# The normed x of five later pieces of work is turned by strided DMA through DRAM in place of TensorE

## The reference, cut to what matters

```python
xn = _layernorm(x)
x = x + _L0_attn_ref(xn, ...) + _L0_ffn_ref(xn, ...)
xn = _layernorm(x)
x = x + _L1_attn_ref(xn, ...) + _L1_ffn_ref(xn, ...)

def _L0_ffn_ref(x, Wg, Wu, Wd, Wr, Ag, Bg, Au, Bu, Ad, Bd):   # 8 experts of rank 16, the best 2 per token
    gate_base = xf @ Wg.T
    up_base = xf @ Wu.T
    base_out = jax.nn.silu(gate_base) * up_base @ Wd.T
    router_logits = xf @ Wr.T
    ...
def _L1_ffn_ref(x, w_gate, w_up, w_down):
    h = jax.nn.silu(x @ w_gate) * (x @ w_up)
    return _sparsify_2to4(h) @ w_down
```

## Time and profile before

| | |
|---|---|
| time, median of 2 runs | 722.21 us (719.66 to 724.76) |
| the profiled execution: its own time, its span | 726.31 us, 724.4 us |
| TensorE busy | 687.9 us, 95% of the span |
| VectorE busy | 517.9 us, 71% |
| ScalarE busy | 374.9 us, 52% |
| GpSimd busy | 138.6 us, 19% |
| DMA queue of SyncE | 20,576 packets, 23.79 MB, 10.0% of 16 engines |
| the chain of work that ended last | PE 69%, DVE 19%, issue 5%, ACT 4%, POOL 2%, DMA 1% |

### The profile page before, as it was taken

The page is one execution under the profiler, slowest core; times in us unless marked ns, Lnnn a source line. Parts: engine busy times, 40 slices in busy tenths (PEclk is TensorE's granted clock), DMA queues, the critical chain, the costliest instruction groups (busy, mean ns, idle before and its releaser), DMA issues.

```text
span 724.4 us, 10585 instructions
## 1 busy us (share of the span) xinstructions
PE 687.9 (95%) x4030; PEld 582.1 (80%) x4030; DVE 517.9 (71%) x933; ACT 374.9 (52%) x773; POOL 138.6 (19%) x129
## 2 busy tenths in 40 slices
PE   3899999969989999999999999999999999999997
PEld 2768888858868788887888878887687888888886
DVE  7726566874876466664666656666769998998997
ACT  4786777744754435444344443445656455354541
POOL 7543453510000001000010000100040323303220
PEclk9989999999999999999999999999999999999999
DMA  5085453000000000000000000050000000000000
GB/s 189 5 290 186 136 142 100 1 1 0 1 1 1 0 1 1 1 0 1 1 1 1 0 1 1 1 233 0 1 1 0 1 1 30 1 29 1 2 30 30
DMA packets 21282, 25.78 MB, mean 36 GB/s; under 512 B 976, under 2 KB 19408, under 8 KB 20464
## 3 DMA queue, kind: packets, MB, share of 16 engines
q1 hardware_dynamic: 20576, 23.79, 10.0%
q10 hardware_dynamic: 656, 1.31, 0.5%
HBM read 22.94 MB, written 2.16 MB: 35 GB/s over the span
## 4 chain that ended last, share of the span: by engine, by line
PE 69%; DVE 19%; issue 5%; ACT 4%; POOL 2%; DMA 1%; DVEq 0%; POOLq 0%; ACTq 0%
PE bank L89 21%; PE bank L91 19%; PE bank L90 19%; DVE l_ring_lo L2451 2%; PE bank L489 2%; DVE l_ge L2432 2%; DVE l_h L2447 2%; DVE l_o L2455 1%; DVE l_h L2404 1%; POOL m_den L825 1%; DVE h_raw L1173 1%; PE bank L465 1%; DVE m_st L903 1%; DVE h_ring_lo L1178 1%; PE bank L1395 1%
## 5 line engine op out<-in xcount | busy, mean ns | idle before, releaser
L1173 DVE TENSOR_TENSOR h_raw<-h_s,bank 128x512 f32<-128x512 f32 x104 | 71.4, 687 | 117.5 <-ACT h_s L1163 102.9
L1163 ACT ACTIVATE h_s<-bank 128x512 f32<-128x512 f32 x104 | 62.2, 598 | 161.6 <-PE bank L91 161.5
L1178 DVE TENSOR_TENSOR h_ring_lo<-h_raw,h_ring_hi 128x512 fp32r<-128x512 f32 x92 | 70.5, 766 | 0.1
L1167 ACT ACTIVATE h_ring_hi<-h_raw 128x512 fp32r<-128x512 f32 x104 | 64.7, 622 | 1.2 <-DVE h_raw L1173 1.2
L90 PE MATMUL bank<-fused_lo,h_ring_hi 128*128 128x256 f32 x208 | 58.8, 283 | 0.0
L89 PE MATMUL bank<-f_yT_hi,mlp_hi 128*128 128x512 f32 x128 | 51.6, 403 | 2.9 <-DVE h_raw L1173 2.9
L2152 ACT ACTIVATE l_s<-bank 128x512 f32<-128x512 f32 x32 | 19.1, 598 | 64.6 <-PE bank L91 64.6
L89 PE MATMUL bank<-l_xT_hi,l_wgu 128*128 128x512 f32 x128 | 51.3, 401 | 0.1
L90 PE MATMUL bank<-l_xT_lo,l_wgu 128*128 128x512 f32 x128 | 50.3, 393 | 0.0
L91 PE MATMUL bank<-l_xT_hi,l_lo 128*128 128x512 f32 x128 | 50.3, 393 | 0.0
L91 PE MATMUL bank<-f_yT_hi,fused_lo 128*128 128x512 f32 x128 | 50.2, 392 | 0.0
(11 more groups left out here) (362 smaller groups left out, 2021.5 us busy)
## 6 DMA issues: line engine op xcount, KB each, us to landing
m_W<-m_scratch SPq DMA_DIRECT2D x16, 512.0 KB, 5.8
fused_raw<-in_fused SPq DMA_DIRECT2D x1, 3584.0 KB, 15.6
res<-in_x SPq DMA_DIRECT2D x4, 512.0 KB, 6.0
fused_raw<-in_fused SPq DMA_DIRECT2D x2, 1024.0 KB, 8.2
l_raw<-in_layer SPq DMA_DIRECT2D x1, 2048.0 KB, 8.7
out_x<-res SPq DMA_DIRECT2D x16, 128.0 KB, 1.9
l_raw<-in_layer SPq DMA_DIRECT2D x1, 1280.0 KB, 11.3
fused_raw<-in_fused SPq DMA_DIRECT2D x1, 1152.0 KB, 5.1
```

The source lines that it names most:

```text
L1163: self.nc.scalar.activation(self.s[u % 2][r, :], gate[r, :], ACT.Silu).then_inc(self.silu.sem, 1)
L1167: self.nc.scalar.activation(self.unit(i, u)[0], self.product(i, u), ACT.Copy).then_inc(self.hi.sem, 1)
L1173: self.nc.vector.tensor_tensor(out=self.product(i, u), in0=self.s[u % 2][r, :], in1=up[r, :], op=ALU.mult).then_inc(self.hidden.sem, 1)
L1178: self.nc.vector.tensor_tensor(out=lo, in0=self.product(i, u), in1=f32(hi), op=ALU.subtract).then_inc(self.lo.sem, 1)
```

## The change

A DRAM tensor `tokens` is added, with 512 rows of 256 for each of eight pieces of x, and two views: `by_token` (partition = token) and `by_column` (partition = feature, the 512 tokens along the row, 256 elements apart in memory). For batches 1 to 3 of L0 and tiles 2 and 3 of L1, SyncE waits until xs is written, stores it to `tokens`, waits for that to land, and issues two loads (one for each 128 features) through `by_column` into `xw`, which lies over xs. ScalarE's `high_x` waits for both loads and reads `xw` in place of the banks; `low_x` too. The transposes of these five are gone, and the wait for `zprod` moves to `router_and_ranks`. `norm_x(i + 1)` moves from u = 15, 16 to u = 11, 12, ahead of `scale_y`. In L1 the norm of tile 2 moves from tile 1's body to tile 0's, behind the last `act_abs`, and that of tile 3 likewise to tile 1's; it now waits for `xT_lo` of the tile before. Batch 0 and tiles 0 and 1 are turned by TensorE as before.

```diff
@@ fused_phase, SyncE
+        for i in range(1, B):
+            sp.wait_ge(xs_ready.sem, xs_ready.at(i, 2))
+            sp.dma_start(g.by_token(i), xs[:, :, :]).then_inc(x_stored.sem, 16)
+            sp.wait_ge(x_stored.sem, x_stored.at(i - 1, 16))
+            for k in range(KD):
+                sp.dma_start(xw[:, k, :], g.by_column(i)[:, k, :], allow_slow_non_contiguous=True).then_inc(x_loaded.sem, 16)
         sp.wait_ge(hid.down.sem, hid.down.at(B - 1, NF))
@@ fused_phase, TensorE
-            if i:
-                pe.wait_ge(zprod.sem, zprod.at(i - 1, 2))
...
-                if u == 2:
+                if u == 2 and i == 0:
                     turn_x(i)
@@ fused_phase, ScalarE
         def high_x(i):
+            if i:
+                act.wait_ge(x_loaded.sem, x_loaded.at(i - 1, 32))
             for k in range(KD):
-                act.wait_ge(xT_t.sem, xT_t.at(i, k + 1))
-                nc.scalar.activation(xT[0][:, k, :], turn_bank[k][:, :], ACT.Copy).then_inc(xT_hi.sem, 1)
+                if i == 0:
+                    act.wait_ge(xT_t.sem, xT_t.at(i, k + 1))
+                nc.scalar.activation(xT[0][:, k, :], xw[:, k, :] if i else turn_bank[k][:, :], ACT.Copy).then_inc(xT_hi.sem, 1)
@@ fused_phase, VectorE
                     if u == 10:
                         mean_square(i + 1)
+                    elif u in (11, 12):
+                        norm_x(i + 1, u - 11)
                     elif u == 14:
                         scale_y(i + 1)
-                    elif u in (15, 16):
-                        norm_x(i + 1, u - 15)
@@ layer1_phase, SyncE
+        turned_x(2)
         for i in range(C):
+            if i == 1:
+                turned_x(3)
@@ layer1_phase, TensorE
-            turn_x(following)
+            if following == 1:
+                turn_x(following)
@@ layer1_phase, ScalarE
             exponentials(i)
-            if i and following is not None:
-                norm(following)
             act_silu(i, GP)
...
                 act_abs(i, GP + 3)
+                if following + 1 < C:
+                    norm(following + 1)
                 for j in range(GP):
                     act_hi(i, j)
```

More of the change, by code:

```diff
@@ L197, in program @@
         g.x_in, g.cols_in, g.bias_in = x_in, cols_in, bias_in
+        g.tokens = nc.dram_tensor("tokens", (B + C, S, D), fp32, kind="Internal").ap()
+        g.by_token = lambda n: g.tokens[n].rearrange("(c p) d -> p c d", p=P)
+        g.by_column = lambda n: g.tokens[n].rearrange("t (k p) -> p k t", p=P)
         l1 = layer1_weights(nc, g, layer1_in)
@@ L1320, in fused_phase @@
     over = Map(nc, spread_at)
+    xw = Map(nc, over.at)("f_xw", [P, KD, S])
     xs, ys = over("f_xs", [P, C, D]), over("f_ys", [P, C, D])
@@ L1345, in fused_phase @@
     xs_ready, xT_t, xT_hi, xT_lo = (sg("f_" + n, 2) for n in ("xs", "xTt", "xThi", "xTlo"))
+    x_stored, x_loaded = sg("f_xst", 16), sg("f_xld", 32)
     lg_ready, lg_copied, lgT, centred, exped = (sg("f_" + n, 1) for n in ("lg", "lgc", "lgT", "cent", "exp"))
@@ L1464, in router_and_ranks @@
             pe.wait_ge(xT_lo.sem, xT_lo.at(i, KD))
+            if i:
+                pe.wait_ge(zprod.sem, zprod.at(i - 1, 2))
             known_weights(i, "ranks")
@@ L1689, in low_x @@
                 dve.wait_ge(xT_hi.sem, xT_hi.at(i, k + 1))
-                nc.vector.tensor_tensor(out=xT[1][:, k, :], in0=turn_bank[k][:, :], in1=f32(xT[0][:, k, :]), op=ALU.subtract).then_inc(xT_lo.sem, 1)
+                nc.vector.tensor_tensor(out=xT[1][:, k, :], in0=xw[:, k, :] if i else turn_bank[k][:, :], in1=f32(xT[0][:, k, :]), op=ALU.subtract).then_inc(xT_lo.sem, 1)
         def low_ranks(i, n):
@@ L1933, in layer1_phase @@
     first, a_at, c_at, d_at = splitting.first, splitting.spots.a, splitting.spots.c, splitting.spots.d
+    xw = Map(nc, g.XN)("l_xw", [P, KD, S])
     xs, o = first.xs, first.spare("l_o", [P, L, D])
@@ L1954, in layer1_phase @@
     x_ready, xT_t, xT_hi, xT_lo = first.x_ready, first.xT_t, first.xT_hi, first.xT_lo
+    x_stored, x_loaded = sg("l_xst", 16), sg("l_xld", 32)
     zprod, zsum, zhi, zlo, back, back_added = rest.zprod, rest.zsum, rest.zhi, rest.zlo, rest.back, rest.back_added
@@ L1981, in _, with turned_x @@
     def _(sp):
+        def turned_x(i):
+            sp.wait_ge(x_ready.sem, x_ready.at(i, 1))
+            sp.dma_start(g.by_token(B + i), xs[:, :, :]).then_inc(x_stored.sem, 16)
+            sp.wait_ge(x_stored.sem, x_stored.at(i - 2, 16))
+            for k in range(KD):
+                sp.dma_start(xw[:, k, :], g.by_column(B + i)[:, k, :], allow_slow_non_contiguous=True).then_inc(x_loaded.sem, 16)
+        turned_x(2)
         for i in range(C):
+            if i == 1:
+                turned_x(3)
             for l in range(L):
@@ L2165, in norm @@
         def norm(i):
-            act.wait_ge(xT_t.sem, xT_t.at(i - 1, KD))
+            if i <= 2:
+                act.wait_ge(xT_t.sem, xT_t.at(i - 1, KD))
+            else:
+                act.wait_ge(xT_lo.sem, xT_lo.at(i - 1, KD))
             if i == 1:
@@ L2175, in high_x @@
         def high_x(i):
+            if i >= 2:
+                act.wait_ge(x_loaded.sem, x_loaded.at(i - 2, 32))
             for k in range(KD):
-                act.wait_ge(xT_t.sem, xT_t.at(i, k + 1))
-                nc.scalar.activation(xTs[i % 2][0][:, k, :], turn_bank[k][:, :], ACT.Copy).then_inc(xT_hi.sem, 1)
+                if i == 1:
+                    act.wait_ge(xT_t.sem, xT_t.at(i, k + 1))
+                nc.scalar.activation(xTs[i % 2][0][:, k, :], xw[:, k, :] if i >= 2 else turn_bank[k][:, :], ACT.Copy).then_inc(xT_hi.sem, 1)
         def copy_first(l):
@@ L2352, in low_x @@
                 dve.wait_ge(xT_hi.sem, xT_hi.at(i, k + 1))
-                nc.vector.tensor_tensor(out=xTs[i % 2][1][:, k, :], in0=turn_bank[k][:, :], in1=f32(xTs[i % 2][0][:, k, :]), op=ALU.subtract).then_inc(xT_lo.sem, 1)
+                nc.vector.tensor_tensor(out=xTs[i % 2][1][:, k, :], in0=xw[:, k, :] if i >= 2 else turn_bank[k][:, :], in1=f32(xTs[i % 2][0][:, k, :]), op=ALU.subtract).then_inc(xT_lo.sem, 1)
         def weigh_experts(n):
```

## The result

The changed kernel takes 932.26 us (median of 928.39 and 936.13) where the kernel before takes 722.21. The ratio is 1.2888, with an interval of 1.2809 to 1.2967: slower, by 210 us.

A forecast was written before the change was run, and what follows sets the result against it. TensorE, 95% busy, was taken to bound the kernel. From 724.4 us, less 5.3 for transposes, plus 96 (L0 waits), 81 (L1 waits) and 15 (slow clock), came 911 us of span, 909 us of time; range 760 to 1,620 us.

The forecast's parts named there:

- What bounds it, and the gain: TensorE, 95% busy, sets the end; removing five groups of eight transposes in L0 and L1 gains 5.3 us.
- The time left: From xs ready to its reader: 44.3 us in L0, 34.6 in L1; with cover 45 and 36.6.
- The packet: Each 4-byte element of the strided loads costs 8.8 ns on its engine: load 36 us, pair 72, chain 77.
- The lower bound of 5.5 ns: Strided loads: packet price with record overlap of 3.3 ns taken off, giving 22.5 us a load, 45 a pair.
- The clock and the cover: Slow TensorE clock adds 3 us after each of five waits, 15 us; TensorE's work covers 1 us (L0), 2 (L1).
- The sum: Whole kernel: 724.4 - 5.3 + 96 + 81 + 15 = 911 us of span, 909 us of time.
- The order: Norms moved ahead of the ring copies in L1 (2.07 us on ScalarE) cost 0, or 4 us if nothing covers them.
- A small packet costs as much as a 512-byte one: Rival on the strided loads: pair 213 us, chain 218, time 1,614 us; chance 0.17, shared with the skill page's price.
- Cheaper than the record: Rival on the strided loads: pair 45 us, chain 50, clock barely falls, time 764 us; chance 0.14.
- In between: Rival on the strided loads: scattered reads cost more than the record, pair 110 to 180 us, time 1,100 to 1,450; chance 0.20.
- Hidden: Rival: neighbours gathered or both loads in one's time (36 us), chain 41 us, time 726, or 717 if all hidden; chance 0.06.
- The estimate of 100 us a load: Strided loads by the skill page's factor of 19 over the crossbar: 200 us a pair, time about 1,550 us.

The follow-up runs named there:

- e3_run16: Changed kernel with loads in runs of 16 floats (64 bytes), x not turned: 719.74 us against 722.05 for the kernel before, ratio 0.9954.
- e1_order: Kernel before with the norms moved to where the change puts them, TensorE's transposes kept: 725.52 us against 722.05, ratio 1.0027.
- e5_first_layer: Changed kernel with the change in L0 alone, L1 as in the kernel before: 834.85 us, one execution.
- e4_two_queues: Changed kernel with the second load of each pair issued from ScalarE's queue: 938.4 us, one execution.
- e2_run2: Changed kernel with loads in runs of 2 floats (8 bytes), half the packets, x not turned: 737.42 us, one execution.
- e7_store_side: Changed kernel with the turning done by four stores of 4-byte pieces to DRAM, loads reading whole rows: 2,393.62 us, one execution.

## Why the prediction was right

Its steps, one by one.

**What bounds it, and the gain.** TensorE sets the end, and a wait ahead of it is added whole: the table of differences above gives 37.7 to 38.2 us for waits of 37.8 to 38.7, and 48.2 and 47.3 for the two of 47.8. The gain of 1.07 us a group was 1.0 (e3_run16).

**The time left.** Taken 44.3 us and 34.6 without cover. Measured: 83.1 - 38.7 = 44.4 from the store's issue to where ScalarE stood idle, and 753.80 - 671.43 - 47.70 = 34.7 in the second layer, whose store went out at 671.43. Both distances came from two rows of the old trace and held to 0.1 us.

**The store** landed in 2.8 us, 3 taken, and the loads followed at once. The rows that answer to the earlier trace rows:

```profile
tokens<-f_xs SPq DMA_DIRECT2D x3, 512.0 KB, 2.8
f_xw<-tokens SPq DMA_DIRECT2D x6, 256.0 KB, 60.1
```

The 60.1 is the median of loads that stand first in line (41.2 us) and second (79.6).

**The packet.** 8.8 ns was taken, and it is the term that was mis-sized: 9.5 ns in the middle of a pair, and over the pair, from its issue at 208.63 to 288.98, 80.4 us / 8,192 = 9.8 ns with the landing in it, where 74 us were taken. The chain is 83 us and not 77. The value lay close, but the step to it was weaker than it looks. The 8.8 ns were the length of a packet's record, and in the changed kernel the records are 1.80 times as long as the packets are apart: 1.801 x 9.5 = 17.1 ns. That the record of a small piece ahead of the work is near the distance of those in a full queue is luck; nothing in the old trace showed it. The lower bound of 5.5 ns, which took some overlap off, went the wrong way. The packet count was exact.

**The clock and the cover.** 15 us were taken for the slow clock behind five waits, less 3 x 0.7 + 2 x 2 = 6.1 of cover, for TensorE works on into the wait. From batch 0's start to the end e3_run16 takes 555.3 us and the kernel before 560.3, so the gain is 5.0; the changed kernel takes 767.5, which is 207.2 more. 207.2 + 5.0 - 210.0 = 2.2 us are left for clock less cover, where 8.9 were taken. The clock was taken rightly: worked out as the prediction did it, length times missing clock, the stretches behind the five waits (0.77, 0.76, 0.72, 0.65 and 0.76 over 11 to 12 us) give 15 us, an estimate. The cover was taken too small: it took some 13 us back and not 6, for TensorE was busy 2.6 to 2.7 us in each wait of the first layer and 4.9 and 4.4 us in those of the second.

**The sum.** Waits without cover: 3 x 32.7 + 2 x 42.4 = 182.9 expected, 210.0 measured, 27 more. Clock less cover: 2.2 in place of 8.9, 6.7 less. The early phase: 5.9 less, by chance of the execution, and no term of the sum. Together 911 + 27.1 - 6.7 - 5.9 = 925.5, and 0.3 for the gain, against a span of 925.7. So part of the closeness is luck, terms of both signs; with the packet's price alone set right, the span would have come out at 938. The other 8.8 us between 909 and 932 are not in the profile: the median was put 2.2 us below the span, as for the kernel before, and the median of the two executions, 7.7 us apart, lies 6.6 above it.

**The order** cost 0 (e1_order). **Waits add** (e5_first_layer).

**The rivals.** *A small packet costs as much as a 512-byte one* would have had a load of 106.5 us; it is 40. The argument for it, that 1.8 packets per ns over all engines were not to be had, is refuted: 118,039 in 70 us are 1.69 per ns, against 0.68 in the densest stretch of before. *Cheaper than the record* is refuted by the same number. *In between* (a pair of 110 us and more) too. *Hidden* fails in both its forms: neighbours are not gathered, since the count is one packet per element, and two loads don't run in the time of one (e4_two_queues). But its threshold, a pair of 40 us for the first layer, was right: with a pair of 41 us (e2_run2) the first layer no longer waits and the second still does.

The Trainium skill, page "VectorE: DVE Perf Modes", section "The three transpose paths", calls the strided copy a trap against the crossbar's transpose, which no run here has; against TensorE's turning, 0.5 us of the path, a load of 40 us bears the warning out. The estimate of 100 us a load, worked out in the prediction from its factor of 19, is 2.5 times what was measured. The section gives the factor for a large stride on the side written, which the prediction left out: the changed kernel writes SBUF without a gap and has its stride on the side read. In e7_store_side the side written has the stride, and the same 65,536 elements take 186 us, 1.9 times the estimate.

What the prediction didn't see is that the cure lies in the start of the chain. It took the place of the norm as given; the same packets, begun 42 us earlier and into space that is free by then, cost nothing in four of the five groups. The fifth, tile 2, was not run that way.

## What to carry to other kernels

A load that turns by strides costs its number of contiguous runs, here 9.0 to 9.6 ns for each on each of 16 engines, whether a run has 4, 8 or 64 bytes: count runs, divide by 16, multiply, and compare with the distance from the producer to the reader. If the chain is longer, the excess is paid once for each group; if the chain can be started early enough, it costs nothing, full DMA engines and all. And don't turn the pattern round without a measurement: the same number of 4-byte pieces cost 4.7 times as much when they were written to DRAM.

## What the runs showed of the hardware

- Scattered 4-byte writes from SBUF to DRAM come 45.1 ns apart on an engine, scattered 4-byte reads 9.5, 8-byte reads 9.0 and 64-byte reads 9.6. Neither theory of e7_store_side had it.
- The recorded length of a small packet is not its price. The engines' share reads 1.80 when full of 4-byte reads and 1.70 with the writes; the price is the time over the count.
- An issue behind such a load holds its engine: 39 us on SP for the second load, and 38.23 for an output behind it. On two queues each issue takes 0.6 to 0.7 us. Here nothing waited for SP; what it costs where something does, no run shows.
- TensorE at full work was granted a clock of 1.00 and was busy 90.94 of 91.00 us beside DMA engines with a share of 1.49. It fell where TensorE itself had waited: 0.58 in a wait, 0.77 over the 11 us behind it.
